# Early loads, resident experts and totals in eight products at the seam of a two-part graph kernel

## The reference

```python
a = einsum('bhnd,bhmd->bhnm', q, k) * scale + (adj + adj)
p = softmax(where(row_nonzero, a, -inf)); p = where(isnan(p), 0, p)
x = layernorm(x + (p @ v) @ Wo.T)
```

```python
top1 = argmax(x.mean(axis=1) @ router_w + router_b)
out = adj @ (x @ expert_w[top1])
mean, var = segment_sum(out)/cnt, segment_sum(out*out)/cnt - mean*mean
y = relu((out - mean[top1]) * rsqrt(var[top1] + 1e-5) * gamma[top1] + beta[top1])
x = layernorm(x + y)
```

## Time and profile before

| | us |
|---|---|
| median of 3 runs (2741.02 to 2743.3) | 2743.18 |
| the profiled execution: its time | 2744.08 |
| the profiled execution: its span, first to last instruction | 2742.3 |
| busy: TensorE, weight loads, VectorE | 2581.8, 2156.2, 2103.7 |
| busy: ScalarE, GpSimd | 1782.1, 889.1 |
| DMA over the span | 197 GB/s |
| first instruction of part two | 2476.8 |

### The profile page before, as it was taken

How to read it: one execution, slowest core, us unless ns; L and a number is a source line. 1 busy time by engine, 2 the same in 40 slices (tenths; PEclk the granted TensorE clock), 3 DMA queues, 4 the chain that set the end, 5 groups by cost and what they waited for, 6 DMA issues and landing times. The chain is left out here.

```text
span 2742.3 us, 61258 instructions
## 1 busy us (share of the span) xinstructions
PE 2581.8 (94%) x20290; PEld 2156.2 (79%) x20290; DVE 2103.7 (77%) x4095; ACT 1782.1 (65%) x6184; POOL 889.1 (32%) x491
## 2 busy tenths in 40 slices
PE   7899999999999999999999999999999999867755
PEld 6788888888888888888888888888888888756644
DVE  5977877877877877877877877877877877844977
ACT  4666666666666666666666666666666666635986
POOL 1132332322322332332322322332332321123776
PEclk9999999999999999999999999999999999987887
DMA  5544544544544544544544544544544544458997
GB/s 214 188 162 180 193 162 171 192 164 170 192 163 178 193 164 177 193 164 170 192 164 170 192 166 176 191 166 176 192 166 169 191 164 165 174 203 327 426 417 307
DMA packets 155053, 540.32 MB, mean 197 GB/s; under 512 B 17586, under 2 KB 50354, under 8 KB 107698
## 3 DMA queue, kind: packets, MB, share of 16 engines
q1 hardware_dynamic: 154802, 536.96, 52.8%
HBM read 427.84 MB, written 109.05 MB: 196 GB/s over the span
## 5 line engine op out<-in xcount | busy, mean ns | idle before, releaser
L604 ACT ACTIVATE prob<-prob,neg_max 128x128 f32<-128x128 f32 x2048 | 792.4, 394 | 5.8 <-DVE abs_max L733 5.8
L370 POOL TENSOR_TENSOR norm<-norm,constants 128x1 f32<-128x1 f32 x128 | 70.5, 551 | 1430.8 <-DVE norm L779 1430.8
L604 ACT ACTIVATION_READ_ACCUMULATOR prob<-prob,neg_max 128x1 f32 x2048 | 396.0, 193 | 0.0
L360 POOL TENSOR_TENSOR moments<-moments,conv 128x1024 f32 x128 | 308.9, 2413 | 267.5 <-ACT conv L655 230.4
L590 ACT ACTIVATE qk<-bank 128x512 f32<-128x512 f32 x256 | 152.8, 598 | 319.2 <-PE bank L379 319.2
L705 DVE SCALAR_TENSOR_TENSOR prob<-bank,adj_in 128x512 f32<-128x512 f32 x512 | 316.9, 681 | 11.2 <-PE bank L379 11.2
L722 DVE TENSOR_TENSOR prob<-prob,inv_sum 128x2048 f32<-128x2048 f32 x128 | 295.7, 2310 | 4.4
L728 DVE TENSOR_REDUCE neg_max<-prob 128x16 f32<-128x2048 f32 x128 | 291.8, 2280 | 0.0
L733 DVE TENSOR_REDUCE abs_max<-prob 128x16 f32<-128x2048 f32 x128 | 291.6, 2278 | 0.0
L597 ACT ACTIVATE probT<-bank 128x512 f32<-128x512 f32 x512 | 265.2, 609 | 26.6 <-PE bank L430 26.6
L346 POOL TENSOR_TENSOR xT_lo<-xT_in,xT_hi 128x1024 fp32r<-128x1024 f32 x62 | 274.9, 4433 | 5.0
(11 more groups left out here) (135 smaller groups left out, 5891.3 us busy)
## 6 DMA issues: line engine op xcount, KB each, us to landing
expert_hi<-expert_hi_scratch SPq DMA_DIRECT2D x125, 1024.0 KB, 4.8
expert_lo<-expert_lo_scratch SPq DMA_DIRECT2D x125, 1024.0 KB, 6.9
x_in<-x SPq DMA_DIRECT2D x128, 256.0 KB, 2.6
x_scratch<-x SPq DMA_DIRECT2D x128, 256.0 KB, 2.4
conv_scratch<-conv SPq DMA_DIRECT2D x128, 256.0 KB, 3.0
conv_in<-conv_scratch SPq DMA_DIRECT2D x32, 1024.0 KB, 9.6
x_in<-x_scratch SPq DMA_DIRECT2D x32, 1024.0 KB, 12.3
out<-x_in SPq DMA_DIRECT2D x32, 1024.0 KB, 13.2
```

The source lines that it names most:

```text
L360: pool.tensor_tensor(acc, acc, conv[:, :, :].rearrange("p k d -> p (k d)"), ALU.add).then_inc(moments_added, 1)
L604: last = act.activation(prob[:, par2, h, :], prob[:, par2, h, :], ACT.Exp, bias=neg_max2[:, par2, h:h + 1], scale=2.0, accum_out=row_sum[: ...
```

## The change

The memory of both parts is laid out by one table. In part two the eight places of the ring lie over tiles of part one that are dead at known points, and one tile, `experts`, with both halves of all four experts, lies over the q, k and v weights and over the high half of xT.

1. *Experts.* SyncE loads experts 0 and 1 in slot 124 and 2 and 3 in slot 126. For graphs 124 to 127 TensorE loads the expert's number into a register and addresses `experts` by it. No expert is loaded for these graphs in slots 128 to 131.
2. *Early loads.* Places 0 to 4 are loaded in slots 126, 128 and 129 (three of them), place 5 after the last slot. Places 6 and 7 are loaded at the start of part two as before.
3. *Refills.* Conv and x1 have semaphores of their own. A conv refill waits only for TensorE's turns; x1's waits for the store, as before. TensorE waits for conv, VectorE for x1. SyncE's part is written out instead of looped.
4. *Totals.* Per kind (sums, squares) four products with a 128x32 block of ones and 512 moved columns, a copy to `row_sums`, four turns.
5. *The last group.* GpSimd's two quarters go to VectorE and ScalarE.

```diff
-        last_expert = {B - 3 + i: (w_hi[k], w_lo[k], ld_last[i]) for i, k in enumerate("qkv")}
+        RESIDENT = B - 4
+            def load_resident(e):
+                sp.wait_ge(qk_done, C * (B // 2))
+                if e >= 2:
+                    sp.wait_ge(v_done, B)
+                for part, src in enumerate((expert_hi_dram, expert_lo_dram)):
+                    sp.dma_start(experts[:, e, part, :, :].bitcast(F32), src[e, :, :, :]).then_inc(ld_all, 16)
+            def load_place(g):
+                for par in range(2):
+                    sp.wait_ge(st_x1[par], 16 * 2 * (g + 1))
+                sp.wait_ge(st_conv, 16 * 4 * (g + 1))
+                sp.dma_start(conv_in[g][:, :], by_token(conv_dram, g * C, C)).then_inc(ld_conv_g[g], 16)
+                sp.dma_start(x1_in[g][:, :], by_token(x1_dram, g * C, C)).then_inc(ld_x1_g[g], 16)
...
+                if isinstance(t, int) and t == B:
+                    sp.wait_ge(scores_done, B)
+                    load_place(1)
+                if isinstance(t, int) and t == B + 1:
+                    sp.wait_ge(turned, C * B)
+                    load_place(2)
+                    sp.wait_ge(pv_done, B)
+                    load_place(3)
+                    sp.wait_ge(conv_done, RESIDENT)
+                    load_place(4)
...
+                        if resident:
+                            pe.wait_ge(ld_all, 32 * E)
+                            pe.wait_ge(expert_known, b + 1)
+                            e = pe.value_load(expert_of[0:1, bass.ds(b, 1)], min_val=0, max_val=E - 1)
+                            def part(k, c):
+                                return experts[:, bass.ds(e, 1), k, c, :].rearrange("p e d -> p (e d)")
...
-            for e in range(E):
-                for j in range(C):
-                    at = (e * 2 + kind) * D + j * P
-                    pe.matmul(bank[kind][:, e * C + j:e * C + j + 1], moments[:, at:at + P], ones[:, :],
-                              start=True, stop=True)
+            for e in range(E):
+                at = (e * 2 + kind) * D
+                last = pe.matmul(bank[kind][Q * e:Q * e + Q, :], ones[:, :].to_broadcast([P, Q]),
+                                 moments[:, at:at + D], start=True, stop=True)
+            last.then_inc(rows_summed, 1)
...
+        def refill_conv(h, r, live):
+            if live(h) and live(h + RING):
+                sp.wait_ge(turned, (h + 1) * C)
+                load_conv(h + RING, r)
+        def group(k, r, live):
...
+            refill_conv(g + 1, (r + 1) % RING, live)
+            if live(g):
+                ends_here = isinstance(g, int) and g == NG - 1
+                sp.wait_ge(pool_finished, (g if ends_here else g + 1) * POOL_TURNS)
...
+                sp.dma_start(by_token(out, g * G, G), x1_in[r][:, :]).then_inc(st_g[r], 16)
+            h, r1 = g - REFILL_LAG, (r - REFILL_LAG) % RING
+            if live(h) and live(h + RING):
+                sp.wait_ge(st_g[r1], 16 * ((k if r >= REFILL_LAG else k - 1) + 1))
+                load_x1(h + RING, r1)
```

More of the change, by code:

```diff
@@ L100, in graph_block_program, with late, place @@
         router = sb("router", [1, 4 * E + 3])
+        p1.close()
+        with nc.sbuf_tensor("experts", [P, E, 2, C, D], F32R) as experts:
+            pass
+        RING = 8
+        def late(name, shape):
+            return ctx.enter_context(nc.sbuf_tensor(name, shape, F32))
+        def place(r):
+            return late(f"conv_in{r}", [P, C * D]), late(f"x1_in{r}", [P, C * D])
+        places = [None] * RING
+        places[6], places[7] = place(6), place(7)
+        bnT = late("bnT", [P, 2, C * D])
+        table_area = late("table_area", [P, 2 * C * D])
+        for r in range(6):
+            places[r] = place(r)
+        conv_in, x1_in = [c for c, _ in places], [x for _, x in places]
         rb, logits, ranked, rank = (router[:, i * E:(i + 1) * E] for i in range(4))
@@ L926, in group @@
                 sp.wait_ge(st_g[r1], 16 * ((k if r >= REFILL_LAG else k - 1) + 1))
-                load(h + RING, r1)
-        for r in range(RING):
-            group(0, r, lambda g: 0 <= g < NG)
-        with sp.Fori(1, NG // RING - 1, 1) as k:
-            for r in range(RING):
-                group(k, r, lambda g: True)
-        for r in range(RING):
-            group(NG // RING - 1, r, lambda g: 0 <= g < NG)
+                load_x1(h + RING, r1)
+        for g in range(NG):
+            group(g // RING, g % RING, lambda g: 0 <= g < NG)
         for r in range(RING):
@@ L993, in group @@
             pool.sem_inc(rstd_seen)
[L994 to L995 removed]
+            for j in range(0 if isinstance(g, int) and g == NG - 1 else POOL_TURNS):
+                pool.tensor_scalar(by_node(x1_in, r)[:, j, :], by_node(x1_in, r)[:, j, :], mean_var[:, r % 2, j, 0:1],
                                    rstd[:, r % 2, j:j + 1], ALU.subtract, ALU.mult).then_inc(pool_finished, 1)
[L998 removed]
+        for r in range(RING):
+            group(0, r, lambda g: 0 <= g < NG)
+        with pool.Fori(1, NG // RING - 1, 1) as k:
+            for r in range(RING):
+                group(k, r, lambda g: True)
+        for r in range(RING):
+            group(NG // RING - 1, r, lambda g: 0 <= g < NG)
     @block.scalar
     def _(act):
+        act.wait_ge(rows_summed, 2)
+        act.activation(row_sums[:, 1, :], bank[1][:, :], ACT.Copy).then_inc(rows_copied[1], 1)
         act.wait_ge(columns_ready, 1)
```

204 lines of the change are left out of this document (111 added, 93 removed).

## The result

The changed kernel takes 2736.11 us (median of 19 runs, 2733.31 to 2742.15); beside it the kernel before took 2741.48 (19 runs). The ratio is 0.998, 95% interval [0.9974, 0.9986]: 5.4 us faster, at the edge of what can be told from no change, and 36 were forecast. The profiled execution has a span of 2734.3 us (before 2742.3), so 8.0 us have to be found in the trace.

What follows compares the result with a forecast made beforehand. DMA bandwidth was taken to bound part two: first store at 2504.6, then 199.5 us for 78 MiB plus 1 and 1 us gives 2706, plus 0.9 is 2707, 36 us faster; VectorE's path 2698.0. Range 2697 to 2724.

Steps and rivals of the forecast that it cites:

- Those turns wait for data: Part two: the 28 us beyond 191.9 us in VectorE's 31 steps are waits for TensorE's turns, which wait for data.
- DMA bandwidth bounds the second part: Part two: a group's 3 MiB take 7.67 us at 410 GB/s against VectorE's 6.19, so removing bytes pays.
- the sum by bytes: Part two from the first store: 78 MiB at 410 GB/s, 199.5 us, plus 1 us first group and 1 us landing.
- The moved tiles: Part one's tiles at new addresses: the prediction gave this no time.
- The block 4.3 us sooner: End of part one: resident experts remove TensorE's load waits, so part two starts at 2472.5; ends 5.8 and 0.
- rival 3: End of part one: early loads delay the store graph 126's copy needs; block at 2478, time 2712; chance 0.10.
- The prologue: Start of part two: totals in eight products, 6.7 us to GpSimd's power instead of 15.8, 9.1 us sooner.
- Rival 2: Start of part two: the eight products run one after another, 12.7 us more, time 2720; chance 0.12.
- The end: Last group: GpSimd's half moves to VectorE and ScalarE; last var_eps to store 3.0 us instead of 5.9.
- Rival 1: Part two: transfers are slow all the way, 379 GB/s, 215.8 us, time 2723; chance 0.15.
- a sign of being wrong: Part two: the forecast is wrong if the DMA rate over the stretch is under 400 GB/s.
- Rival 4: Part two: mixed conv loads, x1 loads and stores drop to 330 GB/s, 247.9 us, time 2755, slower; chance 0.03.

Runs made afterwards that it cites:

- x4_after_act: The changed kernel with ScalarE's loop of part two written out, lookups a group ahead: 2725.70 us, ratio to before 0.9943.
- z1_best: The changed kernel with part one's tiles put back, ScalarE's part-two loop written out and two small prologue moves: 2710.66 us, ratio to before 0.9884.
- x1_layout: The kernel before with only part one's tiles put in the changed kernel's order: 2752.23 us against 2742.42, ratio 1.0036.
- y1_place: The changed kernel with oT, x1, yT and the expert back at the old addresses, wo and others moved down: 2723.28 us, ratio to before 0.9934.
- y2_swap: The kernel before with the expert's and wo's tiles exchanged and nothing else moved: 2749.92 us.
- x3_before_act: The kernel before with ScalarE's loop of part two written out, lookups a group ahead: 2735.12 us against 2742.42, ratio 0.9973.
- z2_mid: The kernel before with the expert's tiles placed below oT, x1 and yT, nothing else moved: 2741.67 us.
- y3_late: The changed kernel with the loads of groups 2 to 4 moved behind the last store of conv: 2749.97 us, ratio to before 1.0028.

## Why the prediction was wrong

- **"Those turns wait for data"** is the step that failed. I read 28 us of VectorE's waits for TensorE as data, because SyncE's waits and a DMA share of 1.01 agreed with it. The place of the waits was in the trace before: 20 of the 28 stand at three loop heads, with ScalarE idle for 8.20 us released by "issue", and only 6.6 at two steps near the end (28 and 30). So VectorE's path in after wasn't 191.9 but 218.2 us of steps, and it ruled. Taking ScalarE's loop out of after gives 10.4 us (x4_after_act).
- **"DMA bandwidth bounds the second part"** was half right: a full DMA and a late consumer stood together. Without ScalarE's loop the kernel before gains 7.3 us and then TensorE waits three times as long for loads, and in z1_best the sum by bytes comes out 3.4 us short of the measured stretch. The early bytes are worth 8 to 11 us.
- **The moved tiles** were a term that I put at nothing, without a reason. They took 10.3 us of part one (x1_layout and after alike).
- **The block 4.3 us sooner**: the waits for expert loads are gone, but the seam gained 1.9 us in after and 2.6 in y1_place. Two terms were wrong. A register load holds TensorE up for 0.7 us, not 0.5. And graph 126's product doesn't hang on graph 125's, as I had it: before, it follows its router's product, which waited 3.73 us for VectorE; in y1_place it starts at 2455.64, and before, less the 1.8 us of the start, at 2455.54. Graph 126's copy then waited for the store, which is rival 3.
- **The prologue**: forecast 9.1 us, measured 9.0 (first turns 10.5 us behind the block, 19.4 before). The eight products took 3.64 us at a granted clock of 0.50, against my 4.2, and the steps behind them 3.2 against 2.5, of which 1.2 are a wait for beta that I hadn't counted: the two errors nearly cancel. Rival 2 is out.
- **The end**: from the last var_eps to the end 10.2 became 7.4, 2.8 us less, and 2.9 were forecast.
- **Rival 1**: over the stretch from 2530 to 2720 after moved 388 GB/s, less than the 400 that I had named as a sign of being wrong. But those are holes and not slow transfers: 412 from 2530 to 2660, then 336 at a share of 0.86. With the heads gone it is 421 from 2530 to 2660 (x4_after_act). That the last 40 us of z1_best have 389 GB/s at a share of 0.99 stays unexplained. The Trainium skill (DMA: Bandwidth & Descriptors, Where 436 GB/s comes from) would have about 358 bind between HBM and SBUF; no run here shows that limit. By it the time would have been 2736, which is what was measured, but for another reason: the DMA had holes.
- **Rival 3** came true: in after graph 126's copy starts 3.7 us behind the end of its products, in x4_after_act 1.7, in y1_place 0.4; by the seams with and without early loads it is some 1.4 us in the mean. **Rival 4**: not seen.

In sum: of the 2736.1 us measured, 12.8 go with the tiles (y1_place; 10.3 of them are seen in part one) and 12.6 with ScalarE's loop and the two moves of the prologue (z1_best against y1_place, 2.4 of them those moves). That leaves 2710.7, or some 2713 without the two moves, which the forecast didn't have, against 2707 forecast.

## What to carry to other kernels

List the steps of the bounding engine one by one before you name what it waits for: a wait that comes every eighth time points at the head of a loop of eight and not at bandwidth, even where the DMA is full. When a forecast time agrees, compare it from a mark shortly ahead of the change: here 1.8 us of a start-up that varies made a wrong term look right. A tile that is moved is a change to every product that reads it, so a reordering of allocations has to be timed alone. And small loads that others need at once go ahead of bulk loads in a queue, or their wait goes behind work that doesn't need them.

## What the runs showed that I had not expected

- The time of the expert's products depends on where the tiles lie: 389 or 396 ns in the rows, with the same shapes and a granted clock of 1.00 (1000 to 1150 us). Moving the expert and wo also slowed products of q whose own tiles stayed (392 to 397 ns, y2_swap).
- Part one repeats to a hundredth of a microsecond once the tiles stand: 2223.31 us from graph 2 to graph 121 in the traces of before, x3_before_act, y1_place, z1_best, z2_mid, and 2233.62 in those of after, x1_layout, x4_after_act. What differs between executions is the start (up to 3.8 us) and the seam.
- The second and third loop heads leave ScalarE idle for 6.6 to 8.2 us in before and after: 2.7 or 3.6 us without any instruction shown, then four register loads in a row, 0.4 to 1.1 us each with gaps between.
- VectorE waited 14.0 us for a transfer of 8 kB that had been issued behind 8 MiB on the same queue (y3_late).
